# Clearing a chunk's buckets in ten row-wise transfers, one with each bucket group, instead of two transfers of seven pieces

## The reference, cut to what matters

```python
h = relu(layernorm(x));  x = x + segment_sum(w[:, None] * h[dst], src) @ weight + bias
h = relu(layernorm(x));  x = x + (1 + eps) * h + segment_sum(relu(h[src] + edge_attr), dst)
h = relu(layernorm(x));  x = x + two rounds of a degree-normalised sum over (src, dst)
h = relu(layernorm(x));  x = x + one such sum the other way round
```

## Time and profile before

| | before |
|---|---|
| median of three runs | 10638.9 us |
| span of the profiled execution, first to last instruction | 8140.1 us |
| own time of the profiled execution | not recorded on its page |
| median less span | 2498.8 us, which no view of the profile shows |
| stage 1: first to last POOL scatter start | 183.7 to 4266.7 us |
| busy share of the span PE, DVE, ACT, POOL | 74%, 60%, 39%, 51% |

### The profile page before, as it was taken

One profiled execution on the slowest core, in us unless ns is written; L12 is line 12 of the kernel. 1 busy time (PEld: TensorE's weight loads), 2 busy tenths in 40 slices (PEclk: granted clock), 3 DMA queues, 4 the chain that ended last, 5 costly groups with the idle time before them and its releaser, 6 DMA issues.

```text
span 8140.1 us, 262325 instructions
## 1 busy us (share of the span) xinstructions
PE 6035.4 (74%) x100233; PEld 5370.6 (66%) x100234; DVE 4891.3 (60%) x7261; ACT 3187.4 (39%) x6331; POOL 4167.1 (51%) x4193
## 2 busy tenths in 40 slices
PE   4666666666666666666656888888599999999997
PEld 3545445444454544545445888888599999999996
DVE  4878778787787877878779989889400111110001
ACT  2444444444444444444346777777200000023332
POOL 0777777777777777777773777777200000000000
PEclk7777677777776777777778999999799999999998
DMA  7888888888888888888866988888887887889999
GB/s 208 265 251 255 255 245 263 246 259 255 245 263 248 256 255 248 261 248 255 251 181 210 290 280 285 285 281 287 239 271 251 287 265 259 266 220 197 201 195 175
DMA packets 1880187, 2026.67 MB, mean 249 GB/s; under 512 B 1014580, under 2 KB 1544532, under 8 KB 1879204
## 3 DMA queue, kind: packets, MB, share of 16 engines
q1 hardware_dynamic: 1432390, 1392.30, 59.8%
q10 hardware_dynamic: 347188, 466.19, 18.8%
q0 software_dynamic: 100000, 158.60, 6.2%
HBM read 1303.01 MB, written 630.27 MB: 238 GB/s over the span
## 4 chain that ended last, share of the span: by engine, by line
PE 32%; POOL 31%; issue 18%; DMA 8%; DVE 7%; ACT 3%; SPq 1%; ACTq 0%; DVEq 0%; POOLq 0%
POOL recB L1320 29%; PE pG L2003 11%; PE pT L2003 3%; PE pG L2057 3%; DMA cA<-stg 3%; PE pG L2044 3%; PE pG L1973 2%; PE pR L2003 2%; DMA recB<-zt 2%; DVE msum L1693 2%; DVE doh L1505 2%; PE pG L1961 1%; PE pT L2029 1%; ACT mpl L2276 1%; PE pG L2029 1%
## 5 line engine op out<-in xcount | busy, mean ns | idle before, releaser
L1320 POOL DMA_INDIRECT recB<-rec,qpos x3125 | 3125.1, 1000 | 1140.3 <-issue 1136.6
L1907 PE MATMUL pT<-soh,doh 128*128 128x128 bf16 x10600 | 1317.5, 264 | 973.2 <-ACT stg L2193 939.8
L2193 ACT CAST stg<-pT 128x512 fp8e4<-128x512 f32 x2650 | 1485.7, 586 | 1031.0 <-PE pT L1907 551.6
L1907 PEld LDWEIGHTS pT<-soh,doh 128*128 128x128 bf16 x10600 | 778.2, 115 | 1074.1 <-ACT stg L2193 1056.6
L2003 PE MATMUL pG<-xw,cl 128*128 128x144 bf16 x13780 | 1051.0, 228 | 123.6 <-DMA xw<-hT 80.6
L2003 PEld LDWEIGHTS pG<-xw,cl 128*128 128x128 fp8e4 x13780 | 913.7, 99 | 125.2 <-issue 125.2
L1505 DVE TENSOR_TENSOR soh<-smd,pG 128x1280 bf16<-128x1280 bf16 x530 | 430.7, 813 | 715.8 <-ACT smd L2175 700.4
L1973 PE MATMUL pG<-mpl,doh 128*128 128x144 bf16 x10388 | 788.0, 231 | 24.1 <-POOL mpl L1341 16.5
L1505 DVE TENSOR_TENSOR doh<-dm,pG 128x2560 bf16<-128x2560 bf16 x530 | 783.6, 1479 | 3.8 <-ACT dm L2251 2.6
L1505 DVE TENSOR_TENSOR doh<-smd,pG 128x2560 bf16<-128x2560 bf16 x530 | 782.6, 1477 | 0.0
L1718 DVE TENSOR_REDUCE ysC<-pG 128x144 f32<-128x432 f32 (+1 forms) x50 | 24.6, 542 | 1192.9 <-PE pG L2003 654.6
(11 more groups left out here) (242 smaller groups left out, 13451.4 us busy)
## 6 DMA issues: line engine op xcount, KB each, us to landing
cl<-cA SPq DMA_DIRECT2D x100, 2880.0 KB, 11.8
recB<-zt ACTq DMA_DIRECT2D x100, 2425.5 KB
brec<-recB SPq DMA_DIRECT2D x477, 495.0 KB
erec<-recB SPq DMA_DIRECT2D x477, 495.0 KB, 5.4
cA<-stg ACTq DMA_DIRECT2D x530, 320.0 KB
drow<-dlD SPq DMA_DIRECT2D x157, 640.0 KB
srowB<-srD SPq DMA_DIRECT2D x265, 320.0 KB, 5.7
pl<-cA SPq DMA_DIRECT2D x65, 1280.0 KB, 6.8
```

What stands on the lines that cost most here:

```text
L1320: p.indirect_dma_start(recF, bass.IndirectOffsetOnAxis(ap=qpos[:, s, c:c + 1], axis=0), rec[:, s, c, :], None).then_inc(s_sc[s], 16)
L1907: ins = t.matmul(B8[6 + (g * 5 + e) % 2][:, h * 256 + b * 128:h * 256 + b * 128 + 128], doh[:, o, 2 * e + b, h * 128:(h + 1) * 128], soh[: ...
L2193: a.copy(stg[:, o, :, e * 256:(e + 1) * 256], B8[6 + (g * 5 + e) % 2][:, :].rearrange("p (h x) -> p h x", h=2), saturate=False).then_inc(e ...
```

## The change

`zt` grows from 7 to 10 records (`GB` is 10). `prefill` now takes the group g and clears the group's buckets (10, or 8 for the last) of each of the 128 rows in one contiguous piece of 990 words (792 for the last). ACT issues one with each of the ten groups, again for chunk K+3, and again none in the last three chunks. SP issues 30 at the start instead of 6. The semaphores `s_pz` are used in turn by even and odd groups, so each counts 5 x 16 = 80 for a chunk, and all waits on them follow. Everything that lies behind `zt` in the on-chip memory moves up by 1152 bytes in each partition.

```diff
-        zt = fix("zt", [128, 7, RB], F32)
+        zt = fix("zt", [128, GB, RB], F32)
...
-        def prefill(a, K, h):
-            a.dma_start(recB[bass.ds(K, 1), :, h * 49:h * 49 + 49, :].rearrange("k s (q j) c -> (k s) q (j c)", j=7),
-                        zt[:, :, :].rearrange("p j c -> p (j c)").unsqueeze(1).to_broadcast([128, 7, 7 * RB])
-                        ).then_inc(s_pz[h], 16)
+        def prefill(a, K, g):
+            nb = nbk(g)
+            a.dma_start(recB[bass.ds(K, 1), :, g * GB:g * GB + nb, :].rearrange("k s j c -> (k s) (j c)"),
+                        zt[:, 0:nb, :].rearrange("p j c -> p (j c)")).then_inc(s_pz[g % 2], 16)
...
-                    for h in range(2):
-                        hold(p, s_pz[h], 48 if first else K * 16 + 16)
+                    for o in range(2):
+                        hold(p, s_pz[o], 240 if first else K * 80 + 80)
...
-                v.wait_ge(s_pz[h], NK * 16)
+                v.wait_ge(s_pz[h], NK * 80)
...
-                if g % 5 == 0 and not (known and K + 3 >= NK):
-                    hold(a, s_pz[g // 5], K * 16 + 48)
-                    prefill(a, K + 3, g // 5)
+                if not (known and K + 3 >= NK):
+                    hold(a, s_pz[o], K * 80 + (240 + g // 2 * 16))
+                    prefill(a, K + 3, g)
...
-                for h in range(2):
-                    prefill(sp, K, h)
+                for g in range(JG):
+                    prefill(sp, K, g)
```

## The result

The changed kernel takes 10726.27 us (median of 4 runs, 10719.71 to 10728.55) against 10641.74 us for the kernel before (4 runs): ratio 1.0074, interval 1.0061 to 1.0086. It is 85 us slower; I had forecast 10,639 us and no change. Of all the executions reported in this document one, of the changed kernel at 11975.5 us with a granted clock of 0.567, stands in no ratio.

The account below looks back on a forecast made before the run. The prediction took POOL's 3,125 scatters with their issue gaps to bound stage 1. ACT, bytes, start and collisions each added 0 (collisions +- 19 us) to 10638.9, giving 10639 us, range 10,600 to 10,678.

Parts of the forecast that it names:

- So POOL never waits in stage 1: Stage 1: POOL's 3,125 scatters, each with its 0.30 us issue gap, set the pace, and POOL waits for nothing else.
- a margin of 13 us: Bucket work behind POOL in stage 1: spare time in each chunk of 78.4 us, read from DVE's wait of 13.0 us.
- The sum of zeros: Whole kernel: ACT, bytes, start and collisions each add 0, collisions +- 19 us, giving 10639 us.
- Positions about 11 us early: Before a POOL slot in stage 1: the positions it needs are ready 11.4 us ahead, and would stay so.
- Eight more issues hidden: ACT's queue in stage 1: eight more clearings at 0.73 us, 5.8 us a chunk, inside the margin; bare 292 us.
- ACT's wait for its stores to `cA`: Stores queued behind a clearing: landing falls to 7.4 us, saving 5 us a chunk and leaving about 2.
- The collisions: POOL's scatters lengthened by DVE's operations in stage 1: 0 expected, 19 us usual size, 57 us bound; faster 13%, slower 10%.
- The start: SP's 30 issues at kernel start instead of 6: 0, hidden in a wait of 27.8 us; bare 9.6 us.
- ACT, hidden: ACT in stage 1: issues less saved store waits, about +1 us a chunk against 13 us spare, so 0.
- The chain as a cause: Rival, stage 1: the clearing is on the critical path, so 163 us would mostly go, 10,476 us; chance 3%.
- The fixed part adds up: Rival, ACT's DMA queue: each transfer's fixed cost, 2.6 us, holds the queue 20.8 us longer a chunk, 11,029 us; chance 2%.
- Stores land late: Rival, ACT's stores behind clearings: landing at 12 us makes 22 us of waits a chunk, 11,040 us; chance 2%.

Follow-up runs that it names:

- one moved: Changed kernel with group 4's clearing issued right behind group 3's, still ten on ACT: 10629.02 us, 1.0026 of the kernel before on the slow course; 1.0005 on the fast.
- e3: Changed kernel's ten row-wise clearings issued on ACT in two lots of five, after groups 0 and 5: 1.0199 of the kernel before, on the fast course.
- f4c: Changed kernel with twenty clearings of five buckets on ACT, two with each group: 11022.3 us, 1.0402 of the kernel before on the slow course; 0.9999 on the fast.
- the last three: Changed kernel with group 4's clearing moved, with SP issuing the clearings, and with twenty clearings: 1.0026, 1.0042, 1.0402 of the kernel before (10601.58 us), slow course.

## Why the prediction was wrong

**The step that failed** is the first: "So POOL never waits in stage 1", and with it "a margin of 13 us". It was read rightly from the profile, but the profile was not of the course of the timed runs. The warning stood in my own sum: the 2498.8 us between span and median "are in no view", and still "I carry them over". In every result since, time and span differ by 2 us. The gap was stage 1, which took 6,560 us instead of 4,080, with POOL waiting 16 to 19 us for the positions before each slot. On that course POOL is behind in every pause, and a shift of the positions passes to the end.

**By its own steps, on the fast course.** The sum of zeros: right, 1.0002. The mean scatter was forecast at 999 +- 6 ns, measured 1004 in the profiled run. DVE's wait, 11 to 14 us a chunk: 707.1 / 51 = 13.9. The last scatter at 4267 +- 20: 4285.9. Positions about 11 us early: 11.4. Eight more issues hidden: right, and ten more on top of those as well. ACT's wait for its stores to `cA` was to fall from 363 to about 100 us and fell to 0.5: the direction was right, the 2 us a chunk left over were too many. The collisions: the ratio's interval is +- 0.0009, 7 us, so they did not cost the 19 us allowed for them. The start: SP's 30 transfers moved nothing that can be told.

**On the slow course.** "ACT, hidden", and with it the whole sum of zeros, is the term that was mis-sized. With ten on ACT a chunk is 1.28 us longer, 1.18 of it against before's chunks with the same late clock in the first pause; with five issues, with one moved, or with SP issuing the loss is smaller by the ratios. So number and place of the clearings on ACT matter; but SP's 1.0042 says that something of the spread clearings costs with nothing on ACT, and the way from a clearing to the positions was not found. The late granted clock, 0.81 us in one pause, was in none of my rivals. It looks like the larger part, and by the kernel before's own late chunks it is about 0.1 us of a chunk. No experiment held the clock fixed, and early and late chunks may differ in more than the clock. Why it rises later was not shown; between early and late chunks of the kernel before DVE's steps start within 0.02 us of each other until 10.7 us after POOL's last scatter, so they don't tell.

**The rivals.** The chain as a cause (10,476 us) fell on both courses: no version was faster beyond its interval. "The fixed part adds up" fell on the fast course: twenty transfers instead of two, 0.9999. The Trainium skill, DMA: Bandwidth & Descriptors, section Anatomy of one DMA — SWDGE (gpsimd) path, has a fixed part of about 2.0 us in each DMA. Added up in the queue that would be 18 x 2.0 = 36 us a chunk for them, an estimate, well over the margin of 13 us; the ratio of 0.9999 shows none of it. "Stores land late" came true in another form, in the two experiments where ACT waited for clearings and not for stores (e3 and f4c). The range's upper end, 10,678, was 48 us short.

**What stays open.** What makes a group follow the slow course. It is the same for all kernels and all runs of a group, and the five groups of the experiments were on five chips, so it may belong to the chip or to anything else that a group shares. The rows show only its form: PE's issue slowed from some 6 us after the start of POOL's slot, and normal again 3 us after its end. No experiment on that was made, nor was the kernel before profiled beside the last three. Open too is how the spread clearings delay the positions, whoever issues them, and why two pauses get shorter when the clock is late in the first.

No version beat the kernel before on either course.

## What to carry to other kernels

Compare the span with the median before anything else; where they differ by more than a few us, the profile is of another course, and its margins are not those of the timed runs. Ask then what the change does on a course with no margin. When one pause of a round has grown, look at the whole round before calling it the loss: here a late clock made one pause 0.81 us longer and the round only 0.17. And look for both cases inside one profile; the kernel before had them side by side. A wait on the landing two transfers back is free only as long as something hides it: back to back it cost 163 us on the fast course, and what I read as the same wait most of 421 us on the slow one.

## What the runs showed of the hardware that was not expected

The same kernel took 8,151 to 8,159 us on some chips and 10,602 to 10,645 on others, with all of the difference in the stage of indirect DMAs. On the slow course PE's idle times between matmuls of one line were 0.5, 1.2 and 1.9 us in the later part of POOL's slots, and 3,653 us in total before that line against 104. The granted clock of TensorE rose either about 8.3 or about 13.4 us after POOL's last scatter in chunks of one and the same execution.
